# First attention layer: bias scaled once per head ahead of the loop, and its addition to the scores and the minimum over keys in one VectorE operation per head

## The reference, cut to what matters

```python
head_scale = jnp.exp2(-jnp.arange(1, N_HEAD + 1, dtype=jnp.float32))
scores = jnp.einsum("bhqd,bhkd->bhqk", q, k) * atten_scale
scores = scores + bias[None, None, :, :] * head_scale[None, :, None, None]
attn = jax.nn.softmax(scores, axis=-1)
out = jnp.einsum("bhqk,bhkd->bqhd", attn, v).reshape(Bq, T1_, N_HEAD * D_HEAD)
return out @ W_out + b_out
```

## Time and profile before

| | us |
|---|---|
| median of 3 runs (lowest, highest) | 2073.33 (2072.45, 2074.62) |
| the profiled execution's own time | 2070.71 |
| its span, first to last instruction | 2069.0 |
| PE busy | 1844.2 (89%) |
| DVE busy | 1313.0 (63%) |
| ACT busy | 998.1 (48%) |
| POOL busy | 609.7 (29%) |

### The profile page before, as it was taken

The page is one execution under the profiler, slowest core; times in us unless marked ns, Lnnn a source line. Parts: engine busy times, 40 slices in busy tenths (PEclk is TensorE's granted clock), DMA queues, the critical chain, the costliest instruction groups (busy, mean ns, idle before and its releaser), DMA issues. The chain is left out here.

```text
span 2069.0 us, 43982 instructions
## 1 busy us (share of the span) xinstructions
PE 1844.2 (89%) x14851; PEld 1661.0 (80%) x14851; DVE 1313.0 (63%) x3669; ACT 998.1 (48%) x2467; POOL 609.7 (29%) x730
## 2 busy tenths in 40 slices
PE   5999999999998399966999999999999379999991
PEld 5888888888886288855888888888887379999991
DVE  3677777787777333334887878777877345555545
ACT  3776766767766133324555455454455133333330
POOL 0013223223223300013334333434341254444420
PEclk9999999999999699987999999999999689999996
DMA  6688001001100299972222111111110142222106
GB/s 207 240 273 273 27 26 46 30 25 38 37 18 31 94 290 298 296 252 88 97 89 92 40 45 46 47 41 46 48 37 12 63 157 91 92 76 82 54 30 251
DMA packets 133982, 213.43 MB, mean 103 GB/s; under 512 B 16766, under 2 KB 84897, under 8 KB 133840
## 3 DMA queue, kind: packets, MB, share of 16 engines
q1 hardware_dynamic: 106448, 147.89, 21.4%
q0 software_dynamic: 23040, 59.58, 9.0%
q10 hardware_dynamic: 4352, 4.20, 0.6%
HBM read 111.88 MB, written 103.68 MB: 104 GB/s over the span
## 5 line engine op out<-in xcount | busy, mean ns | idle before, releaser
L486 POOL DMA_INDIRECT buf<-a_rxn,a_disp x192 | 199.9, 1041 | 254.4 <-DVE comb L871 90.5
L1132 PE MATMUL a_psM<-a_wo,a_oT 128*128 128x256 f32 x1024 | 234.1, 381 | 4.4 <-ACT a_oT L638 1.4
L617 ACT ACTIVATE a_S<-a_S,a_mn 128x128 f32<-128x128 f32 x512 | 198.9, 396 | 68.7 <-DVE a_mn L907 68.7
L1132 PEld LDWEIGHTS a_psM<-a_wo,a_oT 128*128 128x128 f32 x1024 | 191.5, 190 | 35.5 <-issue 3.4
L887 DVE TENSOR_TENSOR a_S<-a_S,a_rz 128x512 f32<-128x512 f32 x256 | 177.3, 693 | 8.8
L81 PE MATMUL e_psH<-e_x_hi,e_w_hi 128*128 128x256 f32 x640 | 182.5, 285 | 0.0
L82 PE MATMUL e_psH<-e_x_lo,e_w_hi 128*128 128x256 f32 x640 | 179.2, 280 | 0.0
L83 PE MATMUL e_psH<-e_x_hi,e_w_lo 128*128 128x256 f32 x640 | 179.2, 280 | 0.0
L81 PE MATMUL a_psP<-a_c_hi,a_wk_hi 128*128 128x256 f32 x512 | 155.7, 304 | 9.1 <-DVE a_c_lo L763 9.1
L81 PE MATMUL a_psP<-a_x_hi,a_wq_hi 128*128 128x256 f32 x512 | 156.9, 306 | 5.2 <-DVE a_x_lo L763 5.2
L1095 PE MATMUL a_psT<-ident,a_S 128*128 128x128 f32 x1024 | 139.3, 275 | 17.8 <-DVE a_S L887 17.8
(11 more groups left out here) (185 smaller groups left out, 4840.9 us busy)
## 6 DMA issues: line engine op xcount, KB each, us to landing
buf<-a_zeros SPq DMA_DIRECT2D x16, 1320.0 KB
buf<-a_zeros SPq DMA_DIRECT2D x16, 1024.0 KB
e_rows<-buf SPq DMA_DIRECT2D x64, 256.0 KB, 3.9
e_w_in<-in_L_ffn_w SPq DMA_DIRECT2D x64, 256.0 KB, 3.3
y<-e_y SPq DMA_DIRECT2D x64, 256.0 KB, 3.1
a_ctx<-in_ctx SPq DMA_DIRECT2D x32, 256.0 KB
e_w_out<-in_L_ffn_w SPq DMA_DIRECT2D x64, 128.0 KB, 3.8
y<-a_zeros SPq DMA_DIRECT2D x32, 256.0 KB, 2.3
```

The costliest lines, as they stand in the source:

```text
L486: g_.indirect_dma_start(out=buf, out_offset=bass.IndirectOffsetOnAxis(ap=disp[:, par, i, k:k + 1], axis=0), in_=rxn[:, par, i], in_offset= ...
L617: ins = a.activation(s[:, h], s[:, h], ACT.Exp, bias=mn[:, u % 2, h:h + 1], scale=-1.0, accum_out=z[:, u % 2, h:h + 1])
L1132: ins = mm(psM[:, 0], oT[:, c], wo[:, c], start=c == 0, stop=c == HP - 1)
```

## The change

A tile `sides` holds the bias times `-2^-(head+1)` for all 16 heads; VectorE fills it once, at the end of `before()`. In `read_scores` each head's SCALAR_TENSOR_TENSOR becomes one `tensor_tensor_reduce`: it writes `psS + sides[head]` and keeps the minimum of the row, which goes to `mn`. The TENSOR_REDUCE goes, and with it the semaphore `s_min`; ACT's exponentials wait for `s_read` instead. VectorE's wait for `s_exp`, which guards the buffer of `mn`, now stands ahead of the four heads, not ahead of the reduce.

```diff
@@ -267,7 +267,8 @@
         else:
-            s_min = sem(L + "min_ready")
+            sides = m.sb(L + "sides", [P, H, P])
+            s_sides = sem(L + "sides_scaled")
@@ -609,7 +610,7 @@
                     if first:
-                        act.wait_ge(s_min, at(g, UG, u + 1))
+                        act.wait_ge(s_read, at(g, UG, u + 1))
@@ -895,16 +896,16 @@
                     ve.wait_ge(s_sc, at(g, WG, u // 2 + 1))
                     if first:
+                        if has(g, u, 2):
+                            ve.wait_ge(s_exp, at(g, UG, u - 1))
+                        settle(ve)
                         for h in range(HU):
                             odd, i = divmod(h, 2)
                             head = (u % UT) * HU + 2 * i + odd
-                            ins = v_.scalar_tensor_tensor(out=s[:, h], in0=t.side[:], scalar=-2.0 ** -(head + 1),
-                                                          in1=psS[:, odd, u % 2 * 2 + i], op0=ALU.mult, op1=ALU.add)
+                            ins = v_.tensor_tensor_reduce(out=s[:, h], in0=psS[:, odd, u % 2 * 2 + i], in1=sides[:, head],
+                                                          scale=1.0, scalar=3.0e38, op0=ALU.add, op1=ALU.min,
+                                                          accum_out=mn[:, u % 2, h:h + 1])
                         ins.then_inc(s_read, 1)
-                        if has(g, u, 2):
-                            ve.wait_ge(s_exp, at(g, UG, u - 1))
-                        ve.wait_ge(s_read, at(g, UG, u + 1))
-                        v_.tensor_reduce(mn[:, u % 2], s, AX, ALU.min).then_inc(s_min, 1)
@@ -988,6 +989,10 @@
                     ve.wait_ge(t.s_rest, 16 * 6)
+                    for head in range(H):
+                        ins = v_.tensor_scalar(sides[:, head], t.side[:], -2.0 ** -(head + 1), None, ALU.mult)
+                    ins.then_inc(s_sides, 1)
+                    ve.wait_ge(s_sides, 1)
                     return
```

## The result

| | before | changed |
|---|---|---|
| median (lowest to highest), us | 2073.97 (2072.45 to 2075.82) | 2061.57 (2060.67 to 2062.85) |
| ratio, 95% interval | | 0.9942 [0.9931, 0.9954] |
| profiled execution, us | 2070.71 | 2062.85 |

The kernel is faster by 12.4 us; forecast were 2064.8 us and a range of 2061 to 2080. The profiled execution of the changed kernel is the slowest of its four, and that of before is faster than the four of the table, so the two traces differ by only 7.9 us. Up to the experts they agree with the medians: the first expert matmul starts 12.6 us earlier than before (699.32 against 711.93).

A forecast was written before the change was run, and what follows sets the result against it. PE bounds the steady groups, waiting some 6.1 us behind DVE's minimum. 6.1 + 0.4 (first group) + 2.0 (last group) = 8.5 us off 2070.71 gives 2062.2, or 2064.8 by the median; range 2061 to 2080.

The forecast's parts named there:

- a unit's read of the scores on DVE: Four heads' additions and minimum on DVE: 1.12 us in place of 1.51, 0.39 shorter; range 0.44 shorter to 0.29 longer.
- step 2's wait: Steady groups: PE's wait for the copied probabilities before the product with the values goes, 4.3 us in all.
- step 3's wait for the context: Steady groups: PE's wait for the copied context before the output projection goes, taken as 1.8 us in all.
- first group: PE waits 1.74 us there for a chain with one read in it; claimed gain 0.4 us.
- last group and what follows up to the experts: DVE sets the pace there; five reads' savings of 0.39 count, 2.0 us, and what follows moves up whole.
- scalings: 16 bias scalings on DVE, at most 3.2 us, fall into its 8.88 us wait for the first scores: cost nothing.
- The read of the minimum: DVE's read after each head's addition: 0.28 us a head in all against 0.196 for the addition, by the match pair.
- The forecast's read of step 0: Last group, step 0: one of the five counted reads, since the way goes through ACT; 0.39 us.
- No gain: Rival: DVE's read costs what ACT's does, a unit stays 1.5 us: 2073; case of 2068 to 2073 had 0.24.
- Slower: Rival: a unit's eight instructions don't overlap, 0.45 us a head, 18 us lost: 2091; case above 0.38 had 0.18.
- The count of operations: A skill rule cited for the slower rival: count operations; eight for five in a unit speaks against the change.
- its signs of being right: Head 0.26 to 0.30 us, less DVE busy time, PE's two waits gone, groups 0.4 to 0.5 shorter, scalings inside DVE's wait.

The follow-up runs named there:

- the run without a minimum: Changed kernel with the minimum left out (constant 0) and a unit's additions done as two instructions of 256 columns: 2061.59 us, ratio 0.9951 to the kernel before.
- the run with two reduces: Changed kernel with two idle 512-column TENSOR_REDUCE per unit added ahead of the release of the exponentials: 2114.20 us, ratio 1.0209 to the kernel before.
- the kernel with the scaled bias alone: Kernel before, with the bias scaled once on DVE and added by a plain TENSOR_TENSOR per head, TENSOR_REDUCE kept: 2082.25 us, ratio 1.0049.
- the run with the late release: Changed kernel with one idle 512-column TENSOR_REDUCE per unit added ahead of the release of the exponentials: 2073.73 us, ratio 1.0001 to the kernel before.
- the runs with 16 and 32 idle instructions: Kernel before, with 16 or 32 scalings that nothing reads added on DVE ahead of the loop: 2084.36 us (ratio 1.0061) and 2078.22 us (1.0023).

## Why the prediction was right, and where its sizes were off

The mechanism is the forecast one. The sum gave 8.5 us, the medians show 12.4, and the two traces 12.6 by the experts' start. Term by term, from PE's start-to-start distances in both traces:

| term | forecast, us | measured, us |
|---|---|---|
| a unit's read of the scores on DVE | 0.39 shorter | 0.66 shorter |
| step 2's wait, 13 groups | 4.3 | 4.3 |
| step 3's wait for the context, 12 groups | 1.8 | 4.6 |
| first group | 0.4 | 0.8 |
| last group and what follows up to the experts | 2.0 | 3.0 |
| scalings | 0 | 0 |
| lost at the loop's three jumps back | not forecast | 0.2 |

**The step that was too small is step 3's wait.** "A start 0.34 after the matmul ahead stands against 0.23 in the free case" took its free case from a place behind matmuls of 512 columns. Behind those of 256, where the wait is, the free start is 0.12 (309.09 to 309.21): eight groups waited 0.22, not 0.11, and the four with a shown wait 0.40 to 0.58. Another 0.07 to 0.10 a group was lost inside the output projection, 3.72 against 3.62, which I had not looked at. The two make 3.6 and 1.1 us on these 12 groups. Besides, the prediction's own figures add up to 1.4 + 0.9 = 2.3, and it took 1.8 without giving a reason.

**The read of the minimum** was the other: I gave it 0.084 a head by the match pair and it costs some 0.016, as it starts together with the next addition (0.212 a head against 0.196). In the steady groups this made no difference: either way both waits go, and PE is the cap, as the run without a minimum shows. The estimate of 0.284 a head, which applied the fixed cost of the Trainium skill, "Vector Engine (DVE) Microarchitecture Reference", section 5.2, to this read as to any instruction, was too high: that cost doesn't carry over to such a read by these rows.

**The last group.** From its first `invert` to its last it went from 27.75 us (640.83 to 668.58) to 25.60, 2.15 shorter. The forecast's read of step 0 lies ahead of these marks: PE's wait for the first probabilities of the last group falls by 0.67.

```profile
640.91 1.14 PE L1108 MATMUL a_psV<-a_PT,a_v 128*64 128x128 f32 x16 [2.04 <-ACT a_PT L629]
...
630.52 1.14 PE L1113 MATMUL a_psV<-a_PT,a_v 128*64 128x128 f32 x16 [1.37 <-ACT a_PT L630]
```

That is one read at its full 0.66. The other four would have given 2.64 between the marks and gave 2.15, as DVE now waits for ACT in more places (0.87 us twice in that stretch). So the account by reads holds but for 0.5 us, and what made the forecast's 2.0 too small is the price of a read.

**The rivals.** No gain: out, the read isn't ACT's. Slower: the mechanism holds (the run with two reduces), the price doesn't. The rule that the prediction cites for it from the Trainium skill, "VectorE: DVE Perf Modes", section "The DRAIN you can't avoid", doesn't hold here in its strict form, that the next operation starts only when the pipe is empty: operations of 285 ns start every 212 ns. The section itself excepts operations that are not held, which the prediction left out. The count of operations misled too: eight instructions take 0.85 us where five took 1.51.

**What no step of the prediction had** is DVE's wait at the start of the loop, by all signs a fetch of the loop's program. It puts 9.0 us of waiting on DVE, at a place where DVE happens to have the slack that the change itself had made. In the kernel with the scaled bias alone it cost 7.5 us. That the forecast was not spoilt by it is luck: with the same wait and a unit of 1.44 us, as in the run with the late release, nothing was gained.

**Of its signs of being right,** two came out by size only in part: a head takes 0.21 us and not 0.26 to 0.30, and a group takes 0.7 us less and not 0.4 to 0.5.

## What to carry to other kernels

Look for the short waits of the engine that sets the pace by its start-to-start distances, against a free place with the same shapes ahead of it: the view of waits showed 4.4 us, 9.0 came back. What counts is when the awaited result is released: 128 more reduces, an estimated 77 us of DVE at 0.60 each, cost 12.7 us up to the experts ahead of the release and 2.1 behind it. After adding instructions to an engine with a loop, look at the first instruction behind its jump back and at the instruction queue's packets while the loop runs.

## What the runs showed of the hardware

**The read of DVE's accumulated minimum hides behind the next instruction.** It lasts 82 ns and adds some 16 ns to a head; ACT's row sum adds 0.19 to 0.20 us to an ACTIVATE of the same size.

**A jump back can cost 2.8 to 4.3 us on DVE.** The stall is there in the kernels in which the instruction queue q14 moves 15 to 19 packets of 8 KB from 260 to 515 us (the changed kernel among them), and is 0.3 to 0.4 us in the two in which it moves none. The row of the changed kernel:

```profile
355.42 0.74 DVE L736 TENSOR_SCALAR a_xn<-x_all,a_mv,a_rstd 128x256 f32 x2 [2.90 <-issue]
```

The Trainium skill, "Runtime: NRT & Kernel Launch", section "Instruction fetch mechanics", has the rule: a taken branch whose target lies outside the two blocks of program that an engine holds has to fetch it first. The packets, which come with every pass only where DVE stalls, agree with it; that it is the alignment of the loop to these blocks which decides, as the runs with 16 and 32 idle instructions and without a minimum suggest, is not shown, since no run placed the loop's code by itself.
